# Three streams of a convolution added up in PSUM, and the order of ScalarE's and VectorE's steps around it

## The reference, in short

```python
kern = kern.at[:, cidx, ih + di, iw + dj].add(weight * frac[None], mode='drop')   # four corners
out = conv(_gn(x), kern, padding 3, stride 1) + bias[None, :, None, None]
_gn(v) = (v - mean) / sqrt(var + 1e-5)      # per image and channel, over H and W
return x + out
```

## Time and profile before

| | |
|---|---|
| time of three runs, median (lowest to highest) | 321.54 us (320.04 to 323.8) |
| profiled execution: whole time, span from first to last instruction | 323.41 us, 321.6 us |
| mean granted TensorE clock | 0.967 of full |
| busy in the span: PE, DVE, ACT, POOL | 287.7, 262.0, 219.4, 174.0 us |
| bytes moved by DMA | 59.09 MB |

### The profile page before, as it was taken

How to read it: one execution, slowest core, us unless ns; L and a number is a source line. 1 busy time by engine, 2 the same in 40 slices (tenths; PEclk the granted TensorE clock), 3 DMA queues, 4 the chain that set the end, 5 groups by cost and what they waited for, 6 DMA issues and landing times.

```text
span 321.6 us, 9687 instructions
## 1 busy us (share of the span) xinstructions
PE 287.7 (89%) x3436; PEld 201.3 (63%) x3436; DVE 262.0 (81%) x358; ACT 219.4 (68%) x327; POOL 174.0 (54%) x339
## 2 busy tenths in 40 slices
PE   5920799799999999999999999999999899999990
PEld 2710466467766667677777677767777577776760
DVE  4359599989978897989797998979897989797221
ACT  2259897966968595959788786969595949471300
POOL 6242747565565839293756655565748393844000
PEclk9975699999999999999999999999999999999997
DMA  8952355979998897979797999999998949398605
GB/s 145 155 105 77 98 148 111 262 165 234 213 222 210 183 259 161 265 160 248 171 255 170 236 203 221 218 208 235 195 249 183 256 97 234 92 242 225 135 2 101
DMA packets 128255, 59.09 MB, mean 184 GB/s; under 512 B 122068, under 2 KB 122068, under 8 KB 128228
## 3 DMA queue, kind: packets, MB, share of 16 engines
q1 hardware_dynamic: 115204, 24.90, 41.6%
q0 software_dynamic: 9312, 33.04, 38.1%
q10 hardware_dynamic: 3712, 0.80, 1.3%
HBM read 12.88 MB, written 12.85 MB: 80 GB/s over the span
## 4 chain that ended last, share of the span: by engine, by line
PE 42%; DMA 10%; POOL 10%; ACT 8%; issue 7%; DVE 5%; ACTq 1%; DVEq 0%; POOLq 0%
PE ps_x L792 12%; PE ps_eo L792 11%; DMA xb<-xs 10%; PE ps_y L792 10%; PE ps_s L792 9%; POOL xn L700 5%; ACT xs L344 4%; POOL xb L669 3%; ACT junk L314 2%; DVE e L434 2%; DVE result L459 2%; POOL rtmp L675 1%; DVE xs L455 1%; ACT m L350 1%; ACT ps_y L360 0%
## 5 line engine op out<-in xcount | busy, mean ns | idle before, releaser
L669 POOL DMA_DIRECT2D xb<-xs x192 | 94.4, 498 | 61.7 <-DVE xs L455 58.8
L792 PE MATMUL ps_eo<-xs,w 128*64 128x392 f16 (+1 forms) x576 | 98.7, 324 | 0.0
L792 PE MATMUL ps_eo<-xb,w 128*64 128x392 f16 (+1 forms) x576 | 98.7, 324 | 0.0
L344 ACT ACTIVATE xs<-e 128x900 f16<-128x900 f32 x48 | 59.2, 1233 | 32.5 <-DVE e L434 31.1
L792 PE MATMUL ps_s<-xb,w 128*64 128x392 f16 (+1 forms) x384 | 69.6, 331 | 4.8 <-DMA xb<-xs 4.8
L792 PE MATMUL ps_s<-xs,w 128*64 128x392 f16 (+1 forms) x384 | 70.6, 331 | 0.5 <-ACT m L350 0.5
L792 PEld LDWEIGHTS ps_eo<-xs,w 128*64 128x64 f16 x576 | 61.6, 109 | 12.8
L792 PEld LDWEIGHTS ps_eo<-xb,w 128*64 128x64 f16 x576 | 61.6, 109 | 12.6
L792 PE MATMUL ps_x<-xs,w 128*64 128x392 f16 x384 | 67.7, 328 | 0.0
L792 PE MATMUL ps_x<-xb,w 128*64 128x392 f16 x384 | 67.7, 328 | 0.0
L455 DVE TENSOR_TENSOR xs<-e,xs 128x900 f16<-128x900 f32 x48 | 60.9, 1269 | 0.0
(11 more groups left out here) (90 smaller groups left out, 461.5 us busy)
## 6 DMA issues: line engine op xcount, KB each, us to landing
xb<-xs POOLq DMA_DIRECT2D x96, 168.8 KB, 4.2
xb<-xs POOLq DMA_DIRECT2D x96, 166.9 KB, 4.6
xraw<-x SPq DMA_DIRECT2D x124, 98.0 KB, 2.8
out<-result SPq DMA_DIRECT2D x124, 98.0 KB, 5.2
xraw<-x ACTq DMA_DIRECT2D x4, 98.0 KB, 4.1
out<-result ACTq DMA_DIRECT2D x4, 98.0 KB, 3.7
wnat<-L_conv_weight POOLq DMA_DIRECT2D x1, 36.0 KB, 3.8
pts<-L_conv_P POOLq DMA_DIRECT2D x2, 1.1 KB, 2.9
```

What stands on the lines that cost most here:

```text
L344: act.activation(halves(par, 0, s, count), stream(s, par, count), ACT.Copy).then_inc(hi_ready, count)
L669: pool.dma_start(dst[32 * g:32 * g + 32, 0:run - line * past], src[32 * f:32 * f + 32, line * past:run]).then_inc(shifted[par][b], DMA)
L792: last = pe.matmul(into[p:p + HALF, :, 0:PER * wide], w[:, n // 2, s, q, t, :], moving.rearrange("p n q m -> p n (q m)"), start=fresh and ...
```

## The change

- ps_s gets two banks. Stream 0 writes bank 0; ScalarE copies it unscaled to bank 1 (`middle`); stream 3 adds to bank 0, stream 6 to bank 1. m11 and outs_0 are gone, OUTS is 6.
- A new ScalarE operation, `gather`, writes eo = ps_eo (streams 1 and 2), scaled, plus bias.
- ps_stat is gone; the folded mean and variance go to four columns of ps_eo's first bank, so TensorE's stream 1 waits until they were read. Mean is folded a unit earlier: mean(u+3) ahead of stream 7.
- VectorE: outs_4(u-1) stands behind the first two differences of unit u+1; mean(u+3) ends the step.
- ScalarE: highs 0 and 1, middle, seed 0, squares(u+2), gather, sums(u+3), highs 2 to 4, root(u+2), high 5, seed 1, normalise(u+2).
- Step 0 (`first`) has an order of its own: ScalarE highs, middle, seed 0, gather, highs 2 and 3, squares(2), highs 4 and 5, sums(3), seed 1, root(2), normalise(2); TensorE folds mean(2) ahead of stream 4, variance(2) ahead of 7 and mean(3) ahead of 8.
- Set-up: the kernel filters are built in ps_x and ps_y, and three zero matmuls are added that mark ps_y and the second bank of ps_s.

The diff without the set-up's renamed tiles and with few unchanged lines:

```diff
--- before.py
+++ after.py
@@ -115,10 +114,10 @@
...
         ps_y = ps("ps_y", [128, 2, 512])
-        ps_s = ps("ps_s", [128, 512])
-        ps_stat = ps("ps_stat", [128, 512])
-        var_ps = ps_stat[:, 0:PER]
-        mean_ps = ps_stat[:, PER:2 * PER]
+        ps_s = ps("ps_s", [128, 2, 512])
+        STAT = 400
+        var_ps = ps_eo[:, 0, STAT:STAT + PER]
+        mean_ps = ps_eo[:, 0, STAT + PER:STAT + 2 * PER]
...
@@ -222,10 +222,8 @@
...
         def bank(s):
-            if s in (0, 3):
-                return ps_s[:, 0:N]
-            if s == 6:
-                return ps_eo[:, 1, 0:N]
+            if s in (0, 3, 6):
+                return ps_s[:, s // 6, 0:N]
...
         def pair_of(t):
@@ -345,17 +343,25 @@
...
             def middle(u, first=False):
                 act.wait_ge(conv_done, NS * u + 1)
+                if first:
+                    act.wait_ge(marked, 3)
+                else:
+                    act.wait_ge(combined, OUTS * (u - 1) + 4)
+                act.activation(bank(6), bank(0), ACT.Copy).then_inc(m11_passed, 1)
+
+            def gather(u, first=False):
+                act.wait_ge(conv_done, NS * u + 3)
                 if not first:
-                    act.wait_ge(combined, OUTS * (u - 1) + 1)
-                act.activation(m11[:, :], bank(0), ACT.Identity, bias=biascol[:, 0:1],
-                               scale=scales[:, 1:2]).then_inc(m11_ready, 1)
+                    act.wait_ge(combined, OUTS * (u - 1) + 4)
+                act.activation(eo[:, :, :], pair_of(ps_eo), ACT.Identity, bias=biascol[:, 0:1],
+                               scale=scales[:, 1:2]).then_inc(eo_ready, 1)
...
             def seed(u, r, k, first=False):
...
                 else:
-                    act.wait_ge(combined, OUTS * (u - 1) + (4, 7)[k])
+                    act.wait_ge(combined, OUTS * (u - 1) + (3, 6)[k])
...
@@ -367,17 +373,28 @@
...
                 seed(u, h, 0, first)
-                if stats:
+                if stats and not first:
                     squares(u + 2, (h + 2) % RING)
+                gather(u, first)
+                if early and not first:
+                    sums(u + 3, (h + 3) % RING, nth)
                 if nxt:
-                    for batch in BATCHES[2:]:
-                        high(u + 1, a, *batch, first=first)
+                    high(u + 1, a, *BATCHES[2], first=first)
+                    high(u + 1, a, *BATCHES[3], first=first)
+                if first:
+                    squares(2, 2)
+                if nxt:
+                    high(u + 1, a, *BATCHES[4], first=first)
+                if stats and not first:
+                    root(u + 2)
+                if nxt:
+                    high(u + 1, a, *BATCHES[5], first=first)
+                if first:
+                    sums(3, 3, nth)
...
                 if stats:
-                    root(u + 2)
-                if early:
-                    sums(u + 3, (h + 3) % RING, nth)
-                if stats:
+                    if first:
+                        root(2)
...
@@ -442,6 +459,8 @@
...
                 dve.wait_ge(last_group_normalised, NORMS * (u + 1))
+                if not isinstance(u, int) or u:
+                    dve.wait_ge(lo_ready, NS * u)
...
@@ -461,19 +480,14 @@
             def twice(ap):
...
 
-            def outs_0(u):
-                dve.wait_ge(conv_done, NS * u + 3)
-                dve.wait_ge(m11_ready, u + 1)
-                add(eo[:, :, :], pair_of(ps_eo), twice(m11[:, :]))
-
             def outs_1(u):
                 dve.wait_ge(conv_done, NS * u + 4)
-                dve.wait_ge(combined, OUTS * u + 1)
+                dve.wait_ge(eo_ready, u + 1)
...
             def outs_2(u, par, nth):
                 dve.wait_ge(conv_done, NS * u + 6)
-                dve.wait_ge(combined, OUTS * u + 2)
+                dve.wait_ge(combined, OUTS * u + 1)
...
@@ -481,43 +495,46 @@
...
             def outs_3(u):
                 dve.wait_ge(conv_done, NS * u + 7)
-                dve.wait_ge(combined, OUTS * u + 1)
+                dve.wait_ge(eo_ready, u + 1)
...
             def outs_4(u, par):
                 dve.wait_ge(conv_done, NS * u + 9)
-                dve.wait_ge(combined, OUTS * u + 5)
+                dve.wait_ge(combined, OUTS * u + 4)
...
 
-            def step(u, h, nth, nxt, stats):
+            def step(u, h, nth, nxt, stats, early, first=False):
...
                     differences(u + 1, a)
-                if stats:
-                    mean(u + 2)
+                if not isinstance(u, int) or u:
+                    outs_4(u - 1, a)
...
                     second_differences(u + 1, 2)
-                outs_0(u)
+                if first:
+                    mean(2)
...
                 outs_1(u)
-                if stats:
+                if stats and not first:
...
                     low(u + 1, a, *BATCHES[3])
-                if nxt:
...
                     low(u + 1, a, *BATCHES[5])
+                if first:
+                    spread(2)
                 outs_3(u)
-                outs_4(u, h)
+                if early:
+                    mean(u + 3)
...
@@ -613,13 +630,14 @@
...
             for u in range(2):
-                step(u, u, 0, True, True)
+                step(u, u, 0, True, True, True, first=u == 0)
...
                 for h in range(2):
-                    step(it * 2 + h, h, it, True, True)
+                    step(it * 2 + h, h, it, True, True, True)
...
                 u = UNITS - 4 + h
-                step(u, u % 2, u // 2, u + 1 < UNITS, u + 2 < UNITS)
+                step(u, u % 2, u // 2, u + 1 < UNITS, u + 2 < UNITS, u + 3 < UNITS)
+            outs_4(UNITS - 1, 1)
...
         def _(pool):
@@ -757,20 +776,23 @@
...
                 for n in range(4):
-                    last = pe.matmul((ps_eo, ps_x)[n // 2][:, n % 2, 0:256],
+                    last = pe.matmul((ps_x, ps_y)[n // 2][:, n % 2, 0:256],
...
             pe.wait_ge(srow_step, 7)
-            pe.matmul(ps_s[:, 128:131], ones[:, :], srow[:, 2:5], start=True, stop=True).then_inc(scales_in_psum, 1)
+            pe.matmul(ps_s[:, 0, 128:131], ones[:, :], srow[:, 2:5], start=True, stop=True).then_inc(scales_in_psum, 1)
...
             pe.wait_ge(scales_ready, 1)
-            for k in range(2):
-                last = pe.matmul(ps_x[:, k, 0:N], zeros[:, 0:128], zeros[:, 0:N], start=True, stop=True)
-            last.then_inc(marked, 1)
+            for t in (ps_x, ps_y):
+                for k in range(2):
+                    last = pe.matmul(t[:, k, 0:N], zeros[:, 0:128], zeros[:, 0:N], start=True, stop=True)
+                last.then_inc(marked, 1)
+            pe.wait_ge(srow_step, 1)
+            pe.matmul(ps_s[:, 1, 0:N], zeros[:, 0:128], zeros[:, 0:N], start=True, stop=True).then_inc(marked, 1)
...
@@ -780,7 +802,7 @@
...
                 order = [(n, q, t) for n in range(3) for q in range(2 if s < NS - 1 else 1) for t in range(2)]
-                fresh = s not in (4, 5, 7, 8)
+                fresh = s < 3
...
@@ -795,34 +817,39 @@
...
 
-            def step(u, par, nth, stats, first=False):
+            def step(u, par, nth, stats, early, first=False):
...
                     if s == 0 and not first:
-                        pe.wait_ge(combined, OUTS * (u - 1) + 2)
-                    if s == 2 and not first:
-                        pe.wait_ge(combined, OUTS * (u - 1) + 5)
+                        pe.wait_ge(combined, OUTS * (u - 1) + 1)
+                    if s == 1:
+                        if not first:
+                            pe.wait_ge(eo_ready, u)
+                        pe.wait_ge(var_ready, u + 2 if stats else UNITS)
+                        pe.wait_ge(negmean_ready, 2 if first else u + 3 if early else UNITS)
                     if s == 3:
-                        pe.wait_ge(m11_ready, u + 1)
-                    if s == 1 and stats:
-                        mean(u + 2)
-                    if s == 5 and stats:
+                        pe.wait_ge(m11_passed, u + 1)
+                    if s == 4 and first:
+                        pe.wait_ge(eo_ready, 1)
+                        mean(2)
+                    if s == (7 if first else 5) and stats:
+                        pe.wait_ge(eo_ready, u + 1)
                         variance(u + 2)
+                    if s == (8 if first else 7) and early:
+                        mean(u + 3)
...
                         pe.wait_ge(seeded, 2 * u + 1)
-                    if s == 6:
-                        pe.wait_ge(combined, OUTS * u + 1)
...
             for u in range(2):
-                step(u, u, 0, True, first=u == 0)
+                step(u, u, 0, True, True, first=u == 0)
...
                 for h in range(2):
-                    step(it * 2 + h, h, it, True)
+                    step(it * 2 + h, h, it, True, True)
...
                 u = UNITS - 4 + h
-                step(u, u % 2, u // 2, u + 2 < UNITS)
```

(26 more changed lines are left out.)

## The result

The changed kernel takes 346.3 us (344.4 to 349.2, four runs) against 321.3 for the kernel before on the same chip: a ratio of 1.077 (1.072 to 1.082). I had forecast 319.7, with a range of 317.2 to 325.2.

What follows compares the result with a forecast made beforehand. TensorE was taken to bound the kernel, in steady work waiting only for the shifted copies xb. Unit 1's start, +0.9, and steady copies, -2.7, gave -1.8 us from the median 321.54: 319.7, range 317.2 to 325.2.

Steps and rivals of the forecast that it cites:

- SyncE's queue sets the pace: Rival: stores and loads take 17.38 us a unit, over TensorE's 16.92, delaying sums; +3.2 us, 324.7; chance 0.2.
- ScalarE's new order: Steady units: gather and sums move ahead, 1/sqrt starts 0.4 us earlier, seed 1 ends at 13.2; stream 7 wants it at 13.9.
- The first sign of being wrong: List of waits: ScalarE's sums waiting for x would show the forecast wrong.
- The landing: SyncE's loads of x: 2.8 us until a load lands, used in the rival on SyncE's queue.
- Unit 0: Step 0's own order ends seed 1 later, so stream 7 starts at 52.85, 2.1 us late.
- Unit 1: Stream 3 waits for copies landing at 62.8 instead of starting at 61.88: +0.9 us, bounds +0.2 and +2.1.
- the half clock: Sign of being wrong: a granted clock for unit 0 other than 0.92; an extra 1.2 GHz stretch costs over a microsecond.
- Copies out of the stores' way (-2.7): Steady units: stores start 1.8 us later, first four copies land in 4.0 to 4.2 us instead of 5.2; -2.7 us.
- VectorE's first difference right behind the normalisation: Steady units: first difference starts when GpSimd's normalisation ends, instead of 1.55 us into the unit.
- GpSimd's port: Rival: lows beside GpSimd's normalisation slow it by 0.8 us a unit; +1.2 us, 322.7; chance 0.1.

Runs made afterwards that it cites:

- the runs with the order or the wait taken away: Changed kernel with sums behind seed 1 from step 1 (332.3 us), seed 1 ahead of sums from step 1 (331.5), or sums reading the unit before's loaded x (328.0).
- the mended kernel: Changed kernel, sums behind seed 1, mean folded at stream 8; step 0: seed 1 behind gather, 1/sqrt ahead of sums, var ahead of last low: 320.6 us (0.996).
- the first run with seed 1 ahead: Changed kernel with seed 1 put ahead of the sums from step 1 on, sums staying ahead of the highs: 331.5 us (1.031).
- the last run with seed 1 ahead: Changed kernel with seed 1 ahead of the sums in all steps, sums ahead of the highs, step 0 as in the mended kernel: 330.0 us (1.024).

## Why the prediction was wrong

*The step that failed* is the price of the first rival, "SyncE's queue sets the pace". I saw that the sums would want x at 6.9 us of the unit instead of 11.6, and asked only what the stores ahead of the loads do to them; so the mechanism hung on SyncE being full, cost a tenth here and there, and ended at 324.7. I had listed the load's own wait, for seed 1, nowhere, and under "ScalarE's new order" let seed 1 end at 13.2 without asking who waits for it besides stream 7. The loads do. The sum of the forecast has no term for it, and it measured 18.0 us in the twelve units. The run with outs_4 back shows that the stores don't matter (343.1), the runs with the order or the wait taken away that the cycle does (332.3, 331.5, 328.0). The first sign of being wrong that I had named, sums waiting for x in the list of waits, is what the list shows.

*The landing.* I took the page's median of 2.8 us. A wait for eight loads ends with the last, beside the copies: 6.2 us in the unit above, 5.7 to 7.7 in the eleven turns. Already the 6.2 is 3.4 us more, in a cycle where each tenth counts.

*Unit 0: right.* 2.1 us late at 52.85, measured 52.90; the mended step 0 took it away (50.26).

*Unit 1: the mechanism right, the size wrong.* +0.9 was forecast at stream 3, with +2.1 as the upper end. It started at 65.03, 3.15 later than at 61.88. The normalisation ended at 56.6, 0.7 before the 57.3 of the forecast, but the last of the four copies took 6.9 us to land, over the 5.2 that I held for the upper end. Loads, delayed with seed 1, were issued beside them from 53.06 to 58.96; in the mended kernel the loads were issued by 52.44, the copies from 55.19, and the last landed in 4.6. Then came a loss that I had named only for unit 0, as a sign of being wrong: the half clock (a mean of 0.53 from 65.5 to 69.1).

*Copies out of the stores' way (-2.7): this mechanism is not borne out either.* I had the last of the first four copies land in 4.0 to 4.2 us instead of 5.2. But 5.2 was one unit's; over units 2 to 14 it took 4.8 on average before the change (3.2 to 6.0), 4.7 in the changed kernel (3.2 to 5.7) and 4.7 in the mended one. So landing gave 0.1 us, not 1, and the longest of the changed kernel, 6.9 in unit 1, was beside loads. The mended kernel gains 2.7 in the steady units, but it is another kernel than the one forecast, and with the last outputs put back it still gains 1.7: that the sizes agree is luck. The Trainium skill ("DMA: Bandwidth & Descriptors", Queues, rings and completion order) has each DMA engine take turns between the queue rows that have work. Read as in the prediction, loads and stores are then alike to a copy and the term is 0; the 4.8 and 4.7 agree with that. The stores did become shorter to issue, 8.3 us for 10.6.

*VectorE's first difference right behind the normalisation, GpSimd's port:* the difference starts at 173.54, 0.1 us behind the normalisation, as forecast. The normalisation takes 3.2 us (3.03 before), not 0.8 more, so that rival played no part.

## What to carry to other kernels

Before moving an operation ahead of another on an in-order engine, list what each of the passed operations releases, loads above all, and what the moved one waits for. If the second leads back to the first, the way round must fit into the units that it now spans: add it up with the landing of the last transfer, not the median (here 6.2 us against 3.2). An engine or a queue that idles in every unit while all wait is a sign of such a cycle, and putting the operation behind the releasing one again was the cure here; look then for who waited for the moved operation's own result.

## What the hardware showed unexpectedly

TensorE waited 1.87 us in unit 1 before the change and kept its full clock, and also after 1.98 us in unit 0 of the changed kernel. After the wait of 2.85 us in unit 1, and of 3.1 us in unit 12 of the first run with seed 1 ahead, the granted clock fell to half (1.2 GHz, matmuls of 0.53 us instead of 0.33) while TensorE was working again, as this window of the changed kernel shows:

```profile
65.50:69.10 3.60, 3.60 (x28) 2.00 (x26) 0.19 (x1) 2.61 (x6) 0.00 (x0) 0.53 1.06 301
```

28 matmuls in 3.60 us, where a steady unit has 216 in 16.92, or 46 in 3.60: that one stretch cost about 1.4 us, more than the wait had grown (from 1.87 to 2.85).

The length of the wait does not tell by itself whether this happens. The clock also fell to half after 1.95 us (unit 1 of the first run with seed 1 ahead), after 2.3, 2.4 and 2.7 us (unit 1 of three other runs) and after this wait of the run with outs_4 back:

```profile
203.33 0.47 PE L812 MATMUL ps_y<-xs,w 128*64 128x392 f16 x1 [1.98 <-ACT ps_y L366]
```

It stayed full after 2.0 us in unit 0 of two runs, after 2.1 in unit 1 of the mended kernel with outs_4 back, and after 2.4 in unit 12 of the last run with seed 1 ahead. Two waits of the same 1.98 us thus went both ways; what decides between them, no run here shows.
